# A gate, up and down projection on one core: where the first batch's blocks, weight sums and largest weight stand in VectorE's order

## The reference, cut to what matters

```python
base = jnp.einsum('btd,od->bto', x, W)
lora_out = jnp.einsum('bter,bte,eor->bto', h, gates, B)     # y = base + 2 * lora_out
gate = jnp.einsum('bsh,mh->bsm', y, W_gate)
up = jnp.einsum('bsh,mh->bsm', y, W_up)
h = jax.nn.silu(gate) * up
out = x + jnp.einsum('bsm,hm->bsh', h, W_down)
```

## Time and profile before

| what | value |
|---|---|
| median of three runs | 1334.74 us |
| the profiled execution's own time | 1336.12 us |
| its span, from the first to the last instruction | 1334.3 us |
| TensorE busy | 1321.6 us (99% of the span) |
| VectorE busy | 795.4 us (60%) |
| ScalarE busy | 408.9 us (31%) |
| GpSimd busy | 133.8 us (10%) |
| mean granted TensorE clock | 0.997 of 2.4 GHz |

### The profile page before, as it was taken

The page is one execution under the profiler, slowest core; times in us unless marked ns, Lnnn a source line. Parts: engine busy times, 40 slices in busy tenths (PEclk is TensorE's granted clock), DMA queues, the critical chain, the costliest instruction groups (busy, mean ns, idle before and its releaser), DMA issues.

```text
span 1334.3 us, 22089 instructions
## 1 busy us (share of the span) xinstructions
PE 1321.6 (99%) x8540; PEld 861.8 (65%) x8540; DVE 795.4 (60%) x1540; ACT 408.9 (31%) x705; POOL 133.8 (10%) x163
## 2 busy tenths in 40 slices
PE   9999989989999999999999999999999999999999
PEld 7854456645667666667666666667766666666666
DVE  7798988579614578763752555557373255545612
ACT  4368845553101344321011233332110122222100
POOL 3200202231000111100000111110000011111000
PEclk9999999999999999999999999999999999999999
DMA  8379985224874878853694578653387456666564
GB/s 302 125 252 361 400 303 187 83 79 177 301 241 128 278 263 296 323 200 125 235 346 146 168 243 273 184 172 106 95 309 273 150 180 187 185 184 205 172 233 137
DMA packets 117528, 287.00 MB, mean 215 GB/s; under 512 B 14128, under 2 KB 16816, under 8 KB 116656
## 3 DMA queue, kind: packets, MB, share of 16 engines
q1 hardware_dynamic: 117136, 285.43, 62.6%
q10 hardware_dynamic: 288, 0.16, 0.0%
HBM read 241.24 MB, written 44.30 MB: 214 GB/s over the span
## 4 chain that ended last, share of the span: by engine, by line
PE 94%; DVE 3%; issue 1%; DMA 0%; POOL 0%; ACT 0%; SPq 0%; DVEq 0%; ACTq 0%; POOLq 0%
PE banks L1034 25%; PE banks L987 22%; PE banks L1057 14%; PE banks L1064 13%; PE banks L781 4%; PE banks L957 2%; PE banks L958 2%; PE banks L833 2%; PE banks L877 1%; PE banks L879 1%; PE banks L878 1%; PE banks L1093 1%; PE banks L874 1%; PE banks L876 1%; PE banks L875 1%
## 5 line engine op out<-in xcount | busy, mean ns | idle before, releaser
L1034 PE MATMUL banks<-y_hi,gu_ring 128*128 128x512 f16 x1504 | 354.0, 379 | 0.0
L1034 PEld LDWEIGHTS banks<-y_hi,gu_ring 128*128 128x128 f16 x1504 | 147.2, 98 | 139.0
L1057 PE MATMUL banks<-h,piece 128*128 128x512 f16 x840 | 188.5, 379 | 0.0
L1933 ACT ACTIVATE sg<-banks,sc 128x512 f32<-128x512 f32 x112 | 76.5, 687 | 215.8 <-DVE banks L1669 154.8
L2179 POOL TENSOR_TENSOR m<-m,m 128x256 f32<-128x256 f32 x96 | 69.8, 727 | 721.4 <-DVE m L1650 721.4
L1057 PEld LDWEIGHTS banks<-h,piece 128*128 128x128 f16 x840 | 82.2, 98 | 89.7
L1672 DVE TENSOR_TENSOR banks<-banks,m 128x256 f32<-128x256 f32 x96 | 41.5, 432 | 137.2 <-PE banks L1034 137.1
L1064 PE MATMUL banks<-h,piece 128*128 128x256 f16 x896 | 106.2, 273 | 0.0
L1064 PEld LDWEIGHTS banks<-h,piece 128*128 128x128 f16 x896 | 87.7, 98 | 19.8
L987 PE MATMUL banks<-y_lo,gu_ring 128*128 128x256 f16 x752 | 97.5, 273 | 0.0
L2062 ACT COPY m<-banks 128x256 f32<-128x256 f32 x96 | 35.4, 369 | 175.6 <-PE banks L987 175.6
(11 more groups left out here) (239 smaller groups left out, 1964.3 us busy)
## 6 DMA issues: line engine op xcount, KB each, us to landing
piece<-down_dram SPq DMA_DIRECT2D x80, 448.0 KB, 5.4
mix_c<-mix_dram SPq DMA_DIRECT2D x84, 384.0 KB, 4.0
piece<-Wd SPq DMA_DIRECT2D x64, 448.0 KB, 5.4
gu_ring<-Wu SPq DMA_DIRECT2D x110, 256.0 KB, 3.2
gu_ring<-Wg SPq DMA_DIRECT2D x108, 256.0 KB, 3.2
mix_a<-mix_dram SPq DMA_DIRECT2D x84, 256.0 KB, 2.7
mix_dram<-mixed SPq DMA_DIRECT2D x28, 640.0 KB, 4.7
wb<-w_dram SPq DMA_DIRECT2D x64, 256.0 KB, 3.6
```

What stands on the lines that cost most here:

```text
L1034: mm = MM(bank, w[:, k, :], y_hi[:, k, :], start=False, stop=(k == KC - 1), skip_group_check=True)
L1057: mm = MM(bank, w[:, k, :], h[:, half * MH + k, 0, :], start=(start and k == 0), stop=False, skip_group_check=True)
L1933: S.activation(sg[:, n % SG, :], banks[:, chunk_bank(b, m, 0), :], ACT.Silu, scale=sc[:, b, 1:2]).then_inc(s_sg, 1)
```

## The change

Four edits, all of which concern batch 0's gate and up:

1. y_sums moves on VectorE from unit 9 to unit 6, where it stands behind weight_sums(7) and ahead of two down sums.
2. In VectorE's unit 15, y_blocks now stands ahead of weight_sums(18).
3. own_weight moves from the end of VectorE's unit 26 to unit 25, between cross_34(26) and complete(25, 0). largest_weight moves from the start of unit 27 to unit 26, between complete(26, 1) and cross_45(27). rescale and late_split stay at the start of unit 27.
4. Chunk 7 of batch 1's x is split together with chunk 6: on ScalarE in unit 25 and on GpSimd in unit 26, ahead of cross_1236(27).

```diff
-    SPLIT_X = {19 + k: k for k in range(KC)}
+    SPLIT_X = {19 + k: (k,) for k in range(KC - 2)}
+    SPLIT_X[25] = (KC - 2, KC - 1)
...
-    Y_SUMS_AT = 9
+    Y_SUMS_AT = 6
...
                     if s == MC - 1:
-
-                        largest_weight()
                         rescale(0)
                         late_split(0, FIRST_LATE)
+                    if s == PLAIN - 1:
+                        dve.wait_ge(s_plain, 1)
+                        y_blocks()
                     if s >= PLAIN - 1:
                         for u in SUM_AT.get(s, ()):
                             weight_sums(u)
-                    if s == PLAIN - 1:
-                        dve.wait_ge(s_plain, 1)
-                        y_blocks()
                     if blocks_next:
                         cross_34(s + 1)
+                    if s == MC - 3:
+                        own_weight()
                     if s >= PLAIN:
                         complete(s, 0)
                         complete(s, 1)
...
+                    if s == MC - 2:
+
+                        largest_weight()
                     if blocks_next:
                         cross_45(s + 1)
...
-                    if s == MC - 2:
-                        own_weight()
...
-                if s in SPLIT_X:
-                    x_high(1, SPLIT_X[s])
+                for k in SPLIT_X.get(s, ()):
+                    x_high(1, k)
...
-                        if s - 1 in SPLIT_X:
-                            x_low(1, SPLIT_X[s - 1])
+                        for k in SPLIT_X.get(s - 1, ()):
+                            x_low(1, k)
```

## The result

| what | before | after |
|---|---|---|
| median of seven runs each | 1334.91 us | 1331.03 us |
| the profiled execution's own time | 1336.12 us | 1330.87 us |
| its span | 1334.3 us | 1329.0 us |
| mean granted TensorE clock of it | 0.997 | 0.998 |

The ratio of after to before is 0.9969 (95%: 0.9958 to 0.9981): the change makes the kernel faster by 2.5 to 5.6 us. In the medians it is 3.9 us, where 6.1 were forecast. An instruction of before has its line number one or two higher in the kernel after (L987 is L988, L1660 is L1662).

The account below looks back on a forecast made before the run. The chain is 94% TensorE, whose two stalls and the slow clock behind them offer 10.7 us at most. 4.35 + 6.1 - 2.95 - 1.4 = 6.1 us gained, from 1334.74 to 1328.6 us, range 1324.0 to 1331.0 us.

Parts of the forecast that it names:

- three large terms: Seam of units 15 and 16, 4.35 us won; mains(1, 3), 6.1 us won; cross_45(27), 2.95 + 1.4 us lost.
- the forecast's own two cases: Behind TensorE's wait for cross_45(27) the clock falls, 1328.6 us, chance 0.46, or does not, 1327.2 us, chance 0.26.
- a rival with another cause: A lost cover at the seam of units 15 and 16, 1332.0 us, chance 0.13; the range reaches to its middle.
- the 1.35 us: TensorE's loss at half clock behind its 3.23 us stall at the seam of units 15 and 16, expected to go.
- 3.0 + 1.35 = 4.35 us: Seam of units 15 and 16: TensorE's stall for y_blocks shrinks from 3.23 to 0.23 us and its 1.35 us of slow clock goes.
- The rival of a lost cover at the seam: Units 15 and 16: VectorE, weight_sums(18) or unit 20's weights late, about 2 us stall plus 1.4 us clock; 1332.0 us, chance 0.13.
- weight_sums(18) fits: Ahead of cross_34(16) on VectorE, 2.6 us of idle time take its 2.40 us, 0.2 us to spare, costing nothing.
- Edit 3, first half: own_weight in VectorE's unit 25 fits into idle time before complete(25, 0) with 0.4 us to spare, costing nothing.
- 5.83 us as a fixed price: On GpSimd, the all-reduce starts 5.83 us after GpSimd is free of other work, ending at 265.28 us.
- the new stall: TensorE waits 2.95 us at unit 27's row 1 for cross_45(27), with 1.4 us of slow clock behind it.
- The rival in which the all-reduce costs no such time: The all-reduce ends near 259.6 us, VectorE does not wait, no new stall: 10.5 us won, 1324.2 us, chance 0.11.
- The second stall: TensorE's 4.7 us wait at mains(1, 3) for GpSimd's low part of a W chunk; with its clock, 6.1 us go.

Follow-up runs that it names:

- both repairs: The kernel after with largest_weight moved behind cross_45(27) and the down sums' four buffers in another order: 1324.86 us, ratio 0.9927 (0.9914 to 0.9941).

## Why the prediction was right, and where it was off

The ratio puts the kernel at 0.9969 x 1334.74 = 1330.6 us on the forecast's own base, near the upper end of the range (1331.0), 2.0 us above the forecast. Its direction and two of its three large terms came out as worked and one did not. That the time is still within the range is in part luck: the forecast's own two cases reach only to 1330.0 us, and the rest of the range was there for a rival with another cause.

**Edits 1 and 2: the step that failed.** VectorE was as forecast: y_blocks at 179.40 us, which is the forecast's 180.18 less the 0.78 us by which this execution was ahead, and 0.23 us of stall, to the hundredth. The clock did not fall there, so the 1.35 us came back. The failing step is "3.0 + 1.35 = 4.35 us": it took the wait that ended last as the only one. TensorE's next block products needed ScalarE's copies, and ScalarE stood in front of them for a store that edit 2 does not touch, since the down sum stands ahead of both y_blocks and weight_sums(18). A stall of 1.51 us took the place of the one that went, and the term measured 2.63 us in the trace. (4.35 less 1.51 is 2.84; the 0.2 us between them is accounted for by no row.) The rival of a lost cover at the seam had such a stall, of 2 us and with the lower clock, but named weight_sums(18) or a late load for it. weight_sums(18) fits: once the copies are on time it ends 0.28 us ahead of cross_34(16), where the forecast had 0.2. What would have shown the true one is in the rows of before: the 7.80 us of idle time ahead of ScalarE's copy, a wait in its code for the stores, and the issue of x at 185.32 us, which marks the last store's landing. By them the copy comes at 185.32 less the 0.60 us of edit 1, that is 184.7, or 183.9 us with the lead of 0.78 taken off; it came at 184.09.

**Edit 3, first half** fitted into VectorE's idle time as forecast, 0.45 us being left ahead of complete(25, 0). Its cost is nothing; so is its worth.

**Edit 4** was costed rightly: GpSimd takes chunks 6 and 7 in one go, cross_1236(27) follows at once, and GpSimd is free at 255.62 instead of 264.87 us. 3.41 us of that are TensorE's lead at unit 27, and the rest is 5.84 us, where the forecast had 5.83.

**The all-reduce.** 5.83 us as a fixed price from GpSimd falling free was the step on which the sign of edit 3 hung. It measured 5.86 us. With it the new stall was 2.80 us against 2.95 forecast, and its clock 1.40 us against 1.4. The rival in which the all-reduce costs no such time falls: its idle time is 5.7 to 6.3 us in all twelve traces of this study.

**The second stall** went, and chunks 4 to 7 caught nobody: 6.26 us in the trace against 6.1. The first rescale starts 4.55 us behind unit 27's row 0 instead of 10.03, 5.5 us earlier where 5.4 was forecast.

**From the trace to the median.** The change's terms in the trace come to 4.5 us, the own times differ by 5.25, the medians by 3.9. The forecast took the median as 1.4 us under the profiled execution, as if that were a fixed offset. It is a matter of which execution was profiled, and it goes with the clock. Of the seven runs of the kernel after, two are at 1329.68 and 1329.77 us with a mean clock of 1.000, five at 1330.87 to 1331.55 with 0.998 or 0.999. The 46 runs of the kernel before that were taken beside the experiments fall in groups too: 17 at 1333.4 to 1334.4 us with 0.999, 18 at 1335.0 to 1335.8 with 0.997, and 11 at 1335.7 to 1336.7 with 0.996. The profiled execution of before, with the low clock behind both stalls, took as long as those of the slowest group. So the difference of two profiled executions overstates the change here. No trace of a faster execution of before was kept, so behind which stall the clock held there is not shown.

**What the forecast had in hand and did not ask** is which edit brings the earlier rescale. It had the new stall at 4.35 us and GpSimd's release 5.83 us earlier. With largest_weight left in unit 27 the all-reduce would have ended at the same 265.28 us, TensorE would have come to mains(1, 3) at 281.96 us, and the chunk at about 281: no wait, and no new stall either. That is edit 4 without edit 3, it needed no row that was not there, and the runs bear it out.

## What to carry to other kernels

When a stall is to be removed, look at every engine that waits ahead of the same work, and at what each waits for in its code, since a wait that now ends second is named by no row. Cost each edit of a bundle alone as well as the sum: here one edit gave 6.1 us and another took 4.2 back. A wait for a slow result goes behind what others need from that engine, and where a price runs from the moment that an engine falls free, as the all-reduce's does here, freeing the engine brings the start forward and readying the input does not.

## What the runs showed of the hardware

- The price of turning GpSimd to the all-reduce, 5.7 to 6.3 us, runs from when GpSimd falls free, while the input may still be missing: with the input at 259.11 us the all-reduce started at 261.67. A second one right behind it started after 0.32 us.
- The granted clock behind a stall of 2.8 us is not the same from one execution to the next. In the profiled execution of the kernel after it was 0.50 behind it. It was 1.00 behind the same stall in the kernel with y_sums in unit 9 (2.79 us) and in that of before + edits 3, 4 (2.82 us), while behind a shorter one, the 2.65 us of before + edit 4 alone, it fell to 0.50 about 1.1 us after TensorE had started again. The stretches that follow the stall in these two, and in the third one a stretch in which the clock was low:

```profile
265.14:267.94 2.80, 2.79 (x13) 1.29 (x14) 2.42 (x6) 1.70 (x3) 0.00 (x0) 1.00 0.00 0
266.66:268.39 1.73, 1.73 (x8) 0.80 (x9) 1.35 (x4) 1.15 (x2) 0.00 (x0) 1.00 0.00 0
185.00:188.00 3.00, 3.00 (x9) 1.12 (x8) 0.00 (x0) 0.40 (x2) 0.00 (x0) 0.50 0.82 235
```

- In the twelve kept traces no low clock follows a stall of TensorE of about 1.5 us or less, and one follows every stall of 3.1 us or more.
- The three kernels without a stall above 1.5 us (largest_weight behind cross_45(27), without edit 3, both repairs) had a mean clock of 1.000 in all 15 of their runs. What decides behind 2.7 to 2.8 us was not tried, and stays open.
